# Products that nobody reads, put into TensorE's program at three places of a vision block (1 core, Trainium2)

## The chip, the cores and the metric

The kernel runs on one core of a Trainium2 chip. The metric is the device time of one execution in microseconds, lower is better. The engines of the core work in parallel and meet through semaphores: TensorE (PE; its weight loads are PEld), VectorE (DVE), ScalarE (ACT), GpSimd (POOL) and SyncE (SP), which issues the DMAs. Each engine takes its own instructions in the order written in the program.

## The reference

32 images of 3 x 96 x 96 are cut into patches of 16 x 16, which makes 36 tokens of 768 numbers for each image, 1152 tokens in all. Everything is float32.

```python
p = _layernorm(p, ln1_g, ln1_b)                       # 768 -> W_proj -> 192
h = _layernorm(einsum('bnd,de->bne', p, W_proj), ln2_g, ln2_b)
q, k, v = ...                                         # 8 heads of 24
attn = softmax(einsum('bnhd,bnhe->bhde', q/|q|, k/|k|) * temp)   # 24 x 24, over channels
h = layernorm(h + einsum('bhde,bnhe->bnhd', attn, v) @ W_proj + b)
logits = (h/|h|) . slots                              # 8 experts x 4 slots
D = softmax(logits, over tokens); C = softmax(logits, over slots)
H = gelu((D . h/|h|) @ W_down + b_down); Y = H @ W_up + b_up
out = layernorm(h + C . Y)
```

## The kernel before

The tokens are cut into 11 groups (`NG`) of three images, 108 tokens, the last of two images, 72 tokens. All buffers are in SBUF; `ps` is the PSUM tensor of eight banks. Each engine has one long program written out by hand.

**Head.** SyncE loads `b1`, `g1` and the token weights `wt`, then for each group the transposed input `xT` (for the products) and the plain input `xs` (for the statistics), with the other weights between. There are four buffers `xs`, so the load of group g from 4 on waits until `x_stats(g - 4)` has been made; the wait stands in SyncE's program behind the load of `xT` of the same group. TensorE's `offset` (L399) multiplies `b1` by `wt` and `column_means` (L407) multiplies the constant matrix `share`, 128 x 128 filled with 1/768 by GpSimd's first memset, by the scaled weights `wg`. VectorE subtracts the means and writes `wc` (L637). TensorE waits for it and then makes `token(g)` (L417), six products per group.

**Phase 1.** For the first nine groups (`P1`) TensorE makes `token(g)` and `turn_h(g - 2)`, while VectorE makes `x_stats` (L649), `x_moments`, `token_out`, `token_stats` and `ln2_norm` in order. GpSimd makes the roots.

**Loop.** Then 17 steps s interleave the stages of different groups on TensorE: `values(s-2)`, `project(s-3)`, `logits(s-5)`, `qk(s)`, `turn_dc(s-6)`, `turn_l(s-5)`, `turn_h`, `token`, `gram(s-1)`, `mix(s-2)`, `turn_xn(s-4)`, `slot_in(s-6)`, `norms(s)`. A stage whose group is not between 0 and 10 is left out, so the last steps are thin: from step 12 on, `qk`, `gram` and `norms` are gone; step 15 has `logits(10)`, `turn_dc(9)`, `turn_l(10)` and `slot_in(9)`, and step 16 has `turn_dc(10)` and `slot_in(10)`. `gram` writes bank 3, which VectorE's `scores` reads and marks with `e2_scaled`. `hidden(0)` and `hidden(1)` (the experts' first product, L554) stand at the end of steps 13 and 14.

The stages that the change touches wait as follows. `turn_xn(g)` (L507) waits for `xn(g)` of VectorE; `slot_in(g)` (L542) waits for `dm(g)` of VectorE and `cT(g)` of ScalarE. In ScalarE's program `take_c(s-6)` is first in a step and `take_slots(s-6)` last, and `gelu(0)` (a table load and eight activations, L1026) stands at the end of step 15, in front of `take_c(10)`.

**End.** After the loop TensorE makes `slot_out(0)`, `slot_out(1)`, `hidden(2)`, and then for each group `slot_out(g)` (L565, writes bank 2 + g % 2) and `combine(g-2)` (L578). VectorE adds and makes the statistics of the last norm, GpSimd the root, ScalarE the result, and SyncE writes it out.

Of the kernel before, what the change touches and what calls it, by code (L numbers as in the profile page):

```python
# [35 lines left out]
NG = (B + GI - 1) // GI  # L36
# [14 lines left out]
def at(stage, g, first=0):  # L51

    if first <= g < NG:
        stage(g)
# [6 lines left out]
def tokens(g):  # L61
    return images(g) * TOK


def build(nc, x, x_t, w_tok, ln1_g, ln1_b, ln2_g, ln2_b, g2col, b2col, w_qk, w_v, w_proj, b_proj, temp, slots, scale,
          w_down, b_down, w_up, b_up, ident_h, imgsel_h, negmask_h, out):
    ctx = ExitStack()
    with ctx:
        def sb(name, shape):
            return ctx.enter_context(nc.sbuf_tensor(name, shape, F32))  # L70

        def sem(name):
            return ctx.enter_context(nc.semaphore(name))
# [11 lines left out]
        share = sb("share", [128, 128])  # L85
# [87 lines left out]
        ps = ctx.enter_context(nc.psum_tensor("ps", [128, 8, 512], F32))  # L173

        def csp():
            return ps[:, 0, 0:D]

        def bwp():
            return ps[:, 1, 0:D]
# [49 lines left out]
        def hp(b, ni):  # L229
            return ps[:, b % 2, 0:2 * ni * NP].rearrange("p (e i s) -> p e i s", e=2, i=ni)  # L230
# [30 lines left out]
        share_set = sem("share_set")  # L261
# [29 lines left out]
        e2_scaled = sem("e2_scaled")  # L291
# [51 lines left out]
        @block.sync  # L343
        def _(sp):
            def load_x(g):
                n = tokens(g)
                o = g * GI * TOK * KC
                sp.dma_start(xT[:, o:o + KC * n], x_t[:, o:o + KC * n]).then_inc(xT_in[g], 16)
                if g >= NB:
                    sp.wait_ge(st1_ready, g - NB + 1)  # L350
                sp.dma_start(xs[0:n, g % NB, :], x[g * GI * TOK:g * GI * TOK + n, :]).then_inc(x_in[g], 16)

            sp.dma_start(g1[:, :], ln1_g).then_inc(ln1_in, 16)
            sp.dma_start(b1[:, :], ln1_b).then_inc(ln1_in, 16)
            sp.dma_start(wt[:, :, :], w_tok.rearrange("(k p) e -> p k e", p=128)).then_inc(wtok_in, 16)
            load_x(0)
            sp.dma_start(ident[:, :], ident_h).then_inc(ident_in, 16)
            load_x(1)
            load_x(2)
            sp.dma_start(g2[:, :], g2col).then_inc(ln2_in, 16)  # L360
            sp.dma_start(b2[:, :], b2col).then_inc(ln2_in, 16)
            sp.dma_start(wqk[:, :, :, :, :].rearrange("p f j h d -> p f (j h d)"), w_qk).then_inc(wqkv_in, 16)
            sp.dma_start(wv[:, :, :, :].rearrange("p f h d -> p f (h d)"), w_v).then_inc(wqkv_in, 16)
            load_x(3)
            sp.dma_start(g2row[:, :], ln2_g.partition_broadcast(128)).then_inc(rows_in, 16)
            sp.dma_start(b2row[:, :], ln2_b.partition_broadcast(128)).then_inc(rows_in, 16)
            sp.dma_start(bprow[:, :], b_proj.partition_broadcast(128)).then_inc(rows_in, 16)
            sp.dma_start(imgsel[:, :], imgsel_h).then_inc(masks_in, 16)
            sp.dma_start(negmask[:, :], negmask_h).then_inc(masks_in, 16)
            sp.dma_start(tempc[:, :], temp).then_inc(attn_in, 16)  # L370
            sp.dma_start(wp[:, :, :], w_proj).then_inc(attn_in, 16)
            for g in range(4, NG):
                load_x(g)
            sp.dma_start(spraw[:, :, :, :].rearrange("p f n q -> p f (n q)"),
                         slots.rearrange("(f p) n q -> p f (n q)", f=2)).then_inc(slots_in, 16)
            sp.dma_start(scl[:, :], scale.broadcast_to([F, 1])).then_inc(slots_in, 16)
            sp.dma_start(wd[:, :, :, :].rearrange("p f n h -> p f (n h)"), w_down).then_inc(experts_in, 16)
            sp.dma_start(bd[:, :], b_down).then_inc(experts_in, 16)
            sp.dma_start(bu[:, :], b_up).then_inc(experts_in, 16)
            sp.wait_ge(cleared, 6)  # L380
            for j in range(4):
                sp.dma_start(wu[32 * j:32 * j + HID, :, :], w_up[j]).then_inc(experts_in, 16)

            ov = out.rearrange("b n d -> (b n) d")
            for g in range(NG):
                sp.wait_ge(o4_ready, g + 1)
                sp.dma_start(ov[g * GI * TOK:g * GI * TOK + tokens(g), :],
                             o4[0:tokens(g), g % NQ, :]).then_inc(out_done[g % NQ], 16)
            for i in range(NQ):
                sp.wait_ge(out_done[i], 16 * len(range(i, NG, NQ)))  # L390


        @block.tensor
        def _(pe):
            def offset():
                pe.wait_ge(ln1_in, 32)
                pe.wait_ge(wtok_in, 16)
                for kc in range(KC):
                    mm = pe.matmul(bwp(), b1[:, kc:kc + 1].broadcast_to([128, 128]), wt[:, kc, :],  # L399
                                   start=kc == 0, stop=kc == KC - 1)  # L400
                mm.then_inc(bwp_ready, 1)

            def column_means():
                pe.wait_ge(share_set, 1)
                for kc in range(KC):
                    pe.wait_ge(wg_ready, kc + 1)
                    mm = pe.matmul(csp(), share[:, :], wg[:, kc, :], start=kc == 0, stop=kc == KC - 1)  # L407
                mm.then_inc(csp_ready, 1)
# [137 lines left out]
            def hidden(b):  # L546
                i0, i1 = HB[b][0] * GI, min(B, HB[b][1] * GI)
                pe.wait_ge(xt_ready, HB[b][1])
                if b >= 2:
                    pe.wait_ge(hb_ready, b - 1)  # L550
                for n in range(NE):
                    j = n % 4
                    for f in range(2):
                        mm = pe.matmul(hp(b, i1 - i0)[32 * j:32 * j + HID, n // 4, :, :], wd[:, f, n, :],  # L554
                                       xt[:, f, i0:i1, n, :], start=f == 0, stop=f == 1,
                                       tile_position=(0, 32 * j))
                mm.then_inc(hp_ready, 1)

            def slot_out(g):
                i0, ni = g * GI, images(g)  # L560
                pe.wait_ge(hb_ready, 1 + sum(g >= e for _, e in HB[:-1]))
                if g >= 2:
                    pe.wait_ge(yt_ready, g - 1)
                for e in range(2):
                    mm = pe.matmul(ytp(g), hb[:, e, i0:i0 + ni, :, :].rearrange("p i n q -> p (i n q)"),  # L565
                                   wu[:, e, :], start=e == 0, stop=e == 1)
                mm.then_inc(ytp_ready, 1)

            def combine(g):
# [6 lines left out]
                if g >= 2:  # L576
                    pe.wait_ge(z2_ready, g - 1)
                pe.matmul(yop(g), cT[0:images(g) * SL, g, 0:tokens(g)], yt[0:images(g) * SL, g % NQ, :],  # L578
                          start=True, stop=True).then_inc(yop_ready, 1)

            offset()
            column_means()
            pe.wait_ge(wc_ready, 1)
            for g in range(P1):
                token(g)
# [8 lines left out]
            for s in range(17):  # L594
                at(values, s - 2)
                at(project, s - 3)
                at(logits, s - 5)
                at(qk, s)
                at(turn_dc, s - 6)
                at(turn_l, s - 5)  # L600
                at(turn_h, s + P1 - 2 - 1, P1 - 2)
                at(token, s + P1 - 1, P1)
                at(gram, s - 1)
                at(mix, s - 2)
                at(turn_xn, s - 4)
                at(slot_in, s - 6)
                at(norms, s)
                if s == NG + 2:
                    pe.wait_ge(experts_in, 16 * (3 + 4))
                    pe.wait_ge(qk_ready, NG)  # L610
                    hidden(0)
                if s == NG + 3:
                    pe.wait_ge(v_ready, NG)
                    hidden(1)
            pe.wait_ge(lnn_ready, NG)
            pe.wait_ge(e2_scaled, NG)
            slot_out(0)
            slot_out(1)
            hidden(2)
# [610 lines left out]
```

## Time and profile before

| | |
|---|---|
| median of 3 runs | 141.82 us (139.89 to 144.46) |
| the profiled execution | 140.0 us, span 138.0 us |
| mean granted TensorE clock | 0.939 |
| TensorE matmul busy | 115.0 us (83%), 1779 instructions |
| VectorE busy | 88.9 us (64%) |
| ScalarE busy | 69.0 us (50%) |
| GpSimd busy | 67.0 us (49%) |
| read from HBM, written | 9.17 MB, 0.88 MB |

The span is the time from the first to the last instruction of the profiled execution; the time of that execution is 2.0 us longer. Line numbers are those of the kernel before. One product in float32 shows as two weight loads (PEld) and two matmuls (PE). The granted clock is given as a share of 2.4 GHz.

### The profile page before, as it was taken

The numbers are of one execution on the slowest core, as the hardware profiler recorded it, in microseconds if no ns is written. First come the engines' busy times: TensorE is split into PE (matmuls) and PEld (weight loads), VectorE is DVE, ScalarE is ACT, GpSimd is POOL, SyncE is SP. The second block draws the span as 40 slices with busy tenths as digits, with TensorE's granted clock in tenths as the row PEclk, the third lists the DMA queues.
The fourth block names the chain that finished last, engine by engine and source line by source line (L and its number), as shares of the span: only waits on it lengthen the run. The fifth ranks groups of instructions, "written<-read, shape, count | busy, mean of one in ns | idle before, by whom it ended". The sixth has DMA issues, their size and how long they took to land.

```text
span 138.0 us, 4819 instructions
## 1 busy us (share of the span) xinstructions
PE 115.0 (83%) x1779; PEld 93.6 (68%) x1779; DVE 88.9 (64%) x380; ACT 69.0 (50%) x234; POOL 67.0 (49%) x158
## 2 busy tenths in 40 slices
PE   0297799999699999999999999997986860999920
PEld 0297799888377868578787796866964630788700
DVE  0211999999643687985857558586987440159980
ACT  3000004242862848648675686846644468763553
POOL 8500277767847428837265382743664000007871
PEclk9999999999999999999999999999999555599995
DMA  1999899988000000000000000000000000000232
GB/s 14 337 293 278 269 305 320 314 319 214 5 7 0 5 0 7 5 0 7 0 5 5 0 5 0 10 5 0 5 0 7 0 0 0 5 0 24 72 89 71
DMA packets 7677, 10.34 MB, mean 75 GB/s; under 512 B 2056, under 2 KB 5032, under 8 KB 7656
## 3 DMA queue, kind: packets, MB, share of 16 engines
q1 hardware_dynamic: 7656, 10.06, 24.2%
q8 instruction: 14, 0.23, 0.7%
q14 instruction: 7, 0.06, 0.1%
HBM read 9.17 MB, written 0.88 MB: 73 GB/s over the span
## 4 chain that ended last, share of the span: by engine, by line
PE 47%; DVE 22%; issue 12%; POOL 10%; ACT 4%; DMA 3%; SPq 1%; POOLq 1%; DVEq 0%; ACTq 0%
DVE st L649 8%; PE ps L565 7%; PE ps L436 6%; PE ps L476 5%; PE ps L496 3%; PE ps L542 3%; PE ps L399 3%; DMA wt<-in_w_tok 3%; PE ps L489 3%; PE ps L519 3%; DVE y L663 3%; PE ps L578 3%; DVE st L671 2%; PE ps L507 2%; PE ps L407 2%
## 5 line engine op out<-in xcount | busy, mean ns | idle before, releaser
L417 PE MATMUL ps<-wc,xT 128*108 128x192 f32 (+1 forms) x132 | 23.0, 327 | 1.5 <-DVE wc L637 1.5
L940 ACT ACTIVATE hT<-ps,b,g 96x108 f32<-96x108 f32 (+1 forms) x22 | 8.4, 430 | 27.9 <-PE ps L426 27.9
L417 PEld LDWEIGHTS ps<-wc,xT 128*108 128x108 f32 (+1 forms) x132 | 20.7, 170 | 2.0 <-DVE wc L637 1.8
L436 PE MATMUL ps<-wqk,hT 96*108 96x384 f32 (+1 forms) x44 | 16.2, 490 | 0.7 <-ACT qp L962 0.7
L1125 POOL TENSOR_SCALAR pw<-mv 108x1 f32<-108x1 f32 (+1 forms) x11 | 3.7, 337 | 21.3 <-DVE mv L780 21.3
L476 PE MATMUL ps<-hT,wv 96*128 96x108 f32 (+1 forms) x88 | 12.5, 284 | 0.0
L1139 POOL TENSOR_SCALAR var<-mv 108x1 f32<-108x1 f32 (+1 forms) x11 | 2.4, 223 | 18.9 <-DVE mv L875 18.4
L950 ACT ACTIVATE sq<-ps 108x384 f32<-108x384 f32 (+1 forms) x11 | 5.4, 490 | 12.4 <-PE ps L436 12.4
L476 PEld LDWEIGHTS ps<-hT,wv 96*128 96x128 f32 x88 | 10.7, 191 | 0.7
L649 DVE BATCH_NORM_STATS2 st<-xs 108x6 f32<-108x384 f32 (+1 forms) x22 | 10.9, 540 | 0.2 <-issue 0.2
L960 ACT ACTIVATE km<-ps,imgsel 108x192 f32<-108x192 f32 (+1 forms) x32 | 11.0, 418 | 0.0
L565 PE MATMUL ps<-wu,hb 128*96 128x192 f32 (+1 forms) x44 | 10.6, 375 | 0.0
L542 PE MATMUL ps<-dm,xn 108*96 108x96 f32 (+1 forms) x44 | 6.7, 284 | 3.9 <-ACT cT L1013 3.9
L1082 POOL TENSOR_SCALAR var<-mv 108x1 f32<-108x1 f32 (+1 forms) x11 | 2.4, 222 | 15.3 <-DVE mv L655 15.3
L436 PEld LDWEIGHTS ps<-wqk,hT 96*108 96x108 f32 (+1 forms) x44 | 6.8, 171 | 4.1 <-issue 1.6
L1035 ACT ACTIVATE o<-z,sh,rstd 108x192 f32<-108x192 f32 (+1 forms) x11 | 6.0, 546 | 6.4 <-DVE sh L880 6.4
L399 PE MATMUL ps<-wt,b 128*128 128x192 f32 x12 | 4.2, 538 | 6.0 <-DMA wt<-in_w_tok 6.0
L496 PE MATMUL ps<-wp,yT 128*108 128x192 f32 (+1 forms) x44 | 9.1, 330 | 0.0
L542 PEld LDWEIGHTS ps<-dm,xn 108*96 108x96 f32 (+1 forms) x44 | 5.6, 194 | 4.3 <-issue 3.6
L834 DVE RECIPROCAL rC<-sC 108x1 f32<-108x1 f32 (+1 forms) x11 | 1.8, 162 | 10.3 <-ACT eD L1006 10.3
L565 PEld LDWEIGHTS ps<-wu,hb 128*96 128x96 f32 (+1 forms) x44 | 7.3, 184 | 1.5 <-issue 0.7
L399 PEld LDWEIGHTS ps<-wt,b 128*128 128x128 f32 x12 | 3.7, 333 | 5.9 <-issue 5.9
(106 smaller groups left out, 304.6 us busy)
## 6 DMA issues: line engine op xcount, KB each, us to landing
xT<-in_x_t SPq DMA_DIRECT2D x10, 324.0 KB, 7.0
xs<-in_x SPq DMA_DIRECT2D x10, 324.0 KB
out<-o SPq DMA_DIRECT2D x10, 81.0 KB
wt<-in_w_tok SPq DMA_DIRECT2D x1, 576.0 KB, 4.2
wqk<-in_w_qk SPq DMA_DIRECT2D x1, 288.0 KB, 8.7
xT<-in_x_t SPq DMA_DIRECT2D x1, 216.0 KB, 7.5
xs<-in_x SPq DMA_DIRECT2D x1, 216.0 KB
wv<-in_w_v SPq DMA_DIRECT2D x1, 192.0 KB, 9.0
```

The source lines that it names most:

```text
L399: mm = pe.matmul(bwp(), b1[:, kc:kc + 1].broadcast_to([128, 128]), wt[:, kc, :], start=kc == 0, stop=kc == KC - 1)
L417: mm = pe.matmul(tokp(g), xT[:, o + kc * n:o + (kc + 1) * n], wc[:, kc, :], start=kc == 0, stop=kc == KC - 1)
L436: mm = pe.matmul(qkp(g), hT[:, f, t0:t0 + tokens(g)], wqk[:, f, :, :, :].rearrange("p j h d -> p (j h d)"), start=f == 0, stop=f == 1)
L476: mm = pe.matmul(vp(g)[:, m, :], wv[:, f, 4 * m:4 * m + 4, :].rearrange("p h d -> p (h d)"), hT[:, f, t0:t0 + tokens(g)], start=f == 0, st ...
L496: mm = pe.matmul(prp(g), yT[:, g % NY, m, 0:images(g), :].rearrange("p i n -> p (i n)"), wp[:, m, :], start=m == 0, stop=m == 1)
L542: mm = pe.matmul(xtlp(g)[:, f, :], xn[0:tokens(g), g, f * F:(f + 1) * F], dm[0:tokens(g), g % NX, 0:images(g) * SL], start=True, stop=True)
L565: mm = pe.matmul(ytp(g), hb[:, e, i0:i0 + ni, :, :].rearrange("p i n q -> p (i n q)"), wu[:, e, :], start=e == 0, stop=e == 1)
L649: ins = dve.bn_stats(st1[0:n, g % 2, h, :], xs[0:n, g % NB, h * (PD // 2):(h + 1) * (PD // 2)])
L940: ins = act.activation(hT[:, f, t0:t0 + tokens(g)], htp(g)[:, f, :], ACT.Identity, bias=b2[:, f:f + 1], scale=g2[:, f:f + 1])
L950: act.activation(sq[0:n, g % 2, :, :, 0:DH].rearrange("p j h d -> p (j h) d"), p, ACT.Square).then_inc(sq_ready, 1)
L960: act.activation(km[0:n, g % NK, i, :], qkp(g)[:, D:2 * D], ACT.Copy, scale=imgsel[0:n, i:i + 1])
L1035: act.activation(o4[0:n, g % NQ, :], z2[0:n, g % NQ, :], ACT.Identity, bias=sh4[0:n, g:g + 1], scale=rstd4[0:n, g:g + 1]).then_inc(o4_read ...
```

## The change

TensorE gets a helper that multiplies `share` by itself, 128 x 128 by 128 x 128, into bank 3, and nobody reads the result. It stands at these places:
- 11 products at the start of the program, behind a new wait for `share_set` (the memset of `share`);
- 3 products between `column_means` and the wait for `wc`;
- in each of the loop steps 12 to 16, 3 products in front of `turn_xn` and 3 in front of `slot_in` (in steps 15 and 16 there is no `turn_xn`, so that six stand together);
- 6 products after the loop, in front of `slot_out(0)`.

The wait for `e2_scaled` of all groups, which stood behind the loop, moves into step 12, since the products write the bank that `scores` reads.

```diff
+            def keep_busy(count, bank):
+                for _ in range(count):
+                    pe.matmul(ps[:, bank, 0:128], share[:, :], share[:, :], start=True, stop=True)
+
...
+            pe.wait_ge(share_set, 1)
+            keep_busy(11, 3)
             offset()
             column_means()
+            keep_busy(3, 3)
             pe.wait_ge(wc_ready, 1)
...
                 at(mix, s - 2)
+                if s == NG + 1:
+                    pe.wait_ge(e2_scaled, NG)
+                if s > NG:
+                    keep_busy(3, 3)
                 at(turn_xn, s - 4)
+                if s > NG:
+                    keep_busy(3, 3)
                 at(slot_in, s - 6)
                 at(norms, s)
...
+            keep_busy(6, 3)
             pe.wait_ge(lnn_ready, NG)
-            pe.wait_ge(e2_scaled, NG)
             slot_out(0)
```

## Rows read from the trace of the kernel before

**Rows 1.** The page's 40 slices of 3.45 us, busy tenths, clock and DMA.

```profile
PE   0297799999699999999999999997986860999920
PEclk9999999999999999999999999999999555599995
DMA  1999899988000000000000000000000000000232
GB/s 14 337 293 278 269 305 320 314 319 214 5 7 0 5 0 7 5 0 7 0 5 5 0 5 0 10 5 0 5 0 7 0 0 0 5 0 24 72 89 71
```

**Rows 2.** Waits of TensorE: us in total, times, longest us.

```profile
PE ps L399 <- DMA wt<-in_w_tok: 6.0, 1, 6.0
PE ps L542 <- ACT cT L1013: 3.9, 2, 3.4
...
PE ps L417 <- DVE wc L637: 1.5, 1, 1.5
```

**Rows 3.** Windows, TensorE alone: us, busy (instructions), granted clock, DMA.

```profile
36.00:40.00 4.00, 2.89 (x51) 1.00 0.01 4
...
100.00:104.00 4.00, 2.99 (x52) 1.00 0.00 0
104.00:108.00 4.00, 2.75 (x48) 0.94 0.02 6
112.00:116.00 4.00, 1.04 (x6) 0.50 0.00 0
116.00:120.00 4.00, 3.01 (x12) 0.50 0.02 4
```

**Rows 4.** Timeline of the head: start us, us, engine, line, operation.

```profile
0.72 0.20 POOL L1068 MEMSET share<- 128x128 f32 x1 [0.29 <-POOLq L1187]
...
5.96 4.18 PE L399 MATMUL ps<-wt,b 128*128 128x192 f32 x12 [5.96 <-DMA wt<-in_w_tok]
...
13.17 1.35 DVE L637 TENSOR_TENSOR wc<-wg,ps 128x1152 f32<-128x1152 f32 x1 [5.76 <-PE ps L407]
...
14.58 3.66 PE L417 MATMUL ps<-wc,xT 128*108 128x192 f32 x21 [1.52 <-DVE wc L637]
```

**Rows 5.** Timeline of narrow stretches, for the distance between starts.

```profile
6.74 0.85 PE L399 MATMUL ps<-wt,b 128*128 128x192 f32 x2
...
42.27 0.50 PE L476 MATMUL ps<-hT,wv 96*128 96x108 f32 x3
```

**Rows 6.** Issue and landing of an input block, and the chain at x_stats(4).

```profile
11.74 1.12 SPq L348 DMA_DIRECT2D xT<-in_x_t  x1
...
xT<-in_x_t SPq DMA_DIRECT2D x1, 324.0 KB, 8.6
...
22.69 0.91 DVE st L649 x2
```

**Rows 7.** Timeline of TensorE in loop steps 12 to 16.

```profile
101.25 0.39 PE L507 MATMUL ps<-ident,xn 108*96 108x108 f32 x2 [0.18 <-DVE xn L803]
...
104.92 0.39 PE L507 MATMUL ps<-ident,xn 108*96 108x108 f32 x2 [0.57 <-DVE xn L803]
...
107.80 0.48 PE L507 MATMUL ps<-ident,xn 72*96 72x72 f32 x2 [0.28 <-DVE xn L803]
...
111.57 0.93 PE L542 MATMUL ps<-dm,xn 108*96 108x96 f32 x4 [0.49 <-ACT cT L1013]
...
116.99 0.88 PE L542 MATMUL ps<-dm,xn 72*96 72x64 f32 x4 [3.44 <-ACT cT L1013]
```

**Rows 8.** The chain that ended last, from the table load on: start us, us.

```profile
112.88 1.28 ACT L1026
...
117.87 2.61 PE ps L565 x8
120.48 0.59 PE ps L554 x32
121.08 0.90 PE ps L565 x4
```

## The prediction

> **What bounds the kernel now.** I read the page by slices first. TensorE is busy nine tenths or more in most of them, the granted clock stands at full until slice 31, at half in slices 32 to 35, and the DMA engines are nearly full from slice 1 to 9 and then empty [rows 1]. So there are three regimes. In the head, TensorE waits 6.0 us for the token weights and the input stream fills the DMA queues. In the middle, TensorE is the chain. At the end its in-order program stops for other engines. The waits of TensorE name the stops: 6.0 us for the weights at L399, 1.5 us for the centred weights at L417, and 3.9 us at L542, 3.4 of it in one piece, for a copy that ScalarE makes behind the first gelu [rows 2].
>
> The clock is next. The windows give it as 1.00 in 100 to 104 and 0.50 in 112 to 120; it fell late in 104 to 108, after stretches in which TensorE was busy 2.99 and 2.75 of 4 us, and was back at full from about 121.2 after some 3.4 us of back-to-back products from 117.8 on [rows 1, 3, 8]. [...] The head shows 1.00 as well, but its products tell otherwise: two starts of L399 are 0.85 - 0.53 = 0.32 us apart, which is 2 x 192 columns at 1.2 GHz, and L417 passes 21 of the same width in 3.66 us, 0.16 us each [rows 4, 5]. The head runs at the lower level until about 12 us; no record before the first change of clock exists there, and the 1.00 of the view is a default, as I read it.
>
> **Price of a product.** Each fp32 product here is two weight loads and two matmuls. The nearest row for "128 columns of weights, 128 streamed" is L476 (128 and 108): three starts span 0.50 us, the last lasts 0.275, so 0.112 us from start to start. Its 108 streamed columns alone would take 0.09, so the load of 128 columns, the same as here, sets it [rows 5]. From below, 2 x 128 columns at 2.4 GHz give 0.107; from above, L399's 192 columns give 0.16. I take 0.112: a product costs 0.22 us at full clock and 0.44 at half. So three cost 0.67 or 1.3, six 1.34 or 2.7, eleven 2.5 or 4.9.
>
> **Head.** `share` is set at 0.92 [rows 4]. Eleven products at the lower level run from 1.0 to 5.9 at most; the weights are there at 5.96 [rows 4]. They cost nothing, and would cost at most 0.1 us. If they lift the clock by 6 us, L399 takes 12 x 0.16 = 1.9 us for 4.2, L407 ends near 10.0 in place of 13.1, and VectorE's `wc` (13.17, 1.35 us) and the first token product move up by 3.0 us. The three products after `column_means` (0.67) lie in TensorE's wait of 1.5 us for `wc` [rows 2, 4]. Cover gone, they would cost 0.67.
>
> How much of the 3.0 us lives on? The input stream stands against it. The transposed block 4 is issued at 11.74 and lands 8.6 us later, at 20.3; the plain block 4 is next in the queue, 324 KB at about 300 GB/s, 1.1 us, so it lands at about 21.4 to 21.8 [rows 1, 6]. VectorE reads it at 22.69 in `x_stats(4)` [rows 6]. It can be read about 1.0 us earlier, not 3.0: VectorE will stand in front of `x_stats(4)` for about 2 us. Behind it the blocks come every 2.1 us and VectorE takes 2.2 a group, so no more is lost. Bounds: 0.8 if the landing is 21.8, 3.0 if the queue, filled earlier, were also emptied earlier. Queues that are full leave little of that. I take **-1.0**, and everything up to the loop's last steps moves by it.
>
> What the lower level in the head is can be set beside a page. The Trainium skill, "TensorE: Matmul & The Clock Gate", Part 1, says that the low clock is the default and activity releases it, which is what the 0.32 and 0.16 us show. The same part says that the ramp costs under 1% of a typical span; by that the head could give back at most 1.4 us here, against 3.0 from the products and 1.0 after the stream. That sides with the smaller number.
>
> **Loop steps 12 to 16.** TensorE issues in order, so products ahead of `turn_xn` and `slot_in` delay all behind them unless TensorE would have waited. The wait on `e2_scaled` costs nothing: the scores of the last group are step 11's work on VectorE, and `mix(10)`, just ahead in step 12, needs what is made from them. At step 12, `turn_xn(8)` stood at 101.25 after a wait of 0.18 [rows 7]; with three products it stands at 101.65, and `slot_in(6)`, 101.48 before, at 102.55: +1.07. `project(10)`, `logits(8)` and `turn_dc(7)` sit behind it. VectorE takes the logits 0.5 later, since it was busy. In step 13 `turn_xn(9)` (104.92 after 0.57 idle [rows 7]) slips by 0.5, `logits(9)` by 1.2, and VectorE's mask and `unit_h1(10)` by 1.0. In step 14 `turn_xn(10)` (107.80) comes at 109.0: +1.2 [rows 7].
>
> From there the clock pays back. If it stays at full, `slot_in(8)` and `hidden(1)` and `logits(10)` take 1.3 us where they took 2.1, even with three products (0.67) between, so `lm(10)` is late by 0.8, not 1.9. Step 15 has six products in one place, 1.34 us, ahead of `slot_in(9)`, which waited 0.49 for its input [rows 7]: it starts 1.4 late, takes 0.34 + drain for 0.93, and ends 1.0 late. ScalarE's table load and `gelu(0)`, 112.88 to 116.6 [rows 8], move by +1.0, and so does `slot_in(10)`, from 116.99 to 118.0. The six products of step 16 lie in its wait of 3.44 us [rows 7] and cost nothing; if that cover went they would cost 1.34.
>
> **In front of the experts' outputs.** `slot_out(0)` has all its inputs when `slot_in(10)` ends, so six products stand fully on the path: +1.34. But the two `slot_out` after them took 2.61 us at half clock [rows 8] and take 1.3 at full, and `slot_in(10)` saves 0.45. `slot_out(2)`, at 121.08 [rows 8], would start at 118.0 + 0.3 + 1.34 + 1.3 + 0.4 (`hidden(2)`) = 121.35. From there to the end nothing is added and the clock is full in both, so this part is **+0.3**, clock kept. If the products bought no clock it would be far more (below).
>
> **Will the clock stay?** Steps 12 to 15 gain 1.34 us of products each, so 2.99 and 2.75 busy become nearly 4, above anything that lost it [rows 3]. But between the last product of step 16 (115.7) and `slot_in(10)` (118.0) TensorE is idle 2.3 us. Before, 1.5 us idle at L417 left the clock up, and 3.4 us stand in a stretch already low, so the answer lies between [rows 2, 3]. If it falls there, it falls in front of the densest part; the only row for its return is the 3.4 us of back-to-back work before 121.2, half of which is lost: +1.7. I give 0.6 to a fall and take **+1.0**.
>
> **Sum.** 140.0 (span 138.0 and 2.0 around it) - 1.0 + 0.3 + 1.0 = 140.3 against the profiled execution. That execution lies 1.8 under the median of 141.82; the three runs and the profiled one average 141.5. I cannot see in one trace what the slower ones lost. Part may be clock, which the products protect, part the input stream, which they don't. I add half, 0.8 to 0.9: **141.2**.
>
> **Rivals.**
> A, forecast (0.50): head capped by the stream, products nearly pay for themselves, half clock for one dense stretch: 139.0 to 143.0.
> B, faster (0.30): the clock holds through the gelu gap and the first input blocks do land earlier, or the slow ones of the runs before were clock. With 2.0 from the head, 140.0 - 2.0 + 0.3 = 138.3. For it: 144.46 against 139.89 is a spread that the clock could make. Against it: DMA near full from 4 us on [rows 1].
> C, slower (0.14): the clock falls near 107 all the same, because what counts is not TensorE's busy time. Then the products run at 0.44. `slot_in(8)` is 3.0 late, six products at half clock ahead of `slot_in(9)` make it 4.9, six ahead of `slot_out(0)` 7.6, less about 1 for an earlier return: 140.0 - 1.0 + 6.6 = 145.6. It decides if the granted clock is 0.5 before 113. For it: a stretch of 2.99 was near a fall and one of 2.89 was not, so busy time is a poor measure.
> D (0.06): the clock holds, but nothing of the head survives the stream, and the products cost what they save: within 0.5 of before.
>
> **Chances and range.** About 2% is what a measurement of this kernel can tell. Faster than 139.0 needs B or the lower edge of A: 0.24. Slower than 144.7 is C and a rest of A: 0.15. Between, 0.61. The range takes A with its bounds, most of B and not the core of C: 138.0 to 144.2. The likeliest case's own range is 139.0 to 143.0.
>
> **What would show it.** Starts of L399 0.16 us apart; `wc` near 10.2; VectorE idle about 2 us in front of `x_stats(4)`, read at 21.5 to 21.8; `turn_xn(10)` some 1.2 later relative to the loop; a granted clock of 1.00 to at least 115; table load of `gelu(0)` near 113.9 less 1.0; 1.34 us of products directly ahead of L565. A first `x_stats(4)` under 21, or a clock of 0.5 before 113, makes the prediction wrong, the one to the fast side and the other to the slow.

## The result: slower by 3.5%

| | before | changed |
|---|---|---|
| median | 140.85 us (139.43 to 144.46, 4 runs) | 144.68 us (143.05 to 148.24, 4 runs) |
| ratio | | 1.0346, 95% interval 1.0247 to 1.0445 |
| profiled execution, span | 140.0, 138.0 | 144.64, 142.6 |
| mean granted clock | 0.939 | 0.963 |
| TensorE busy | 115.0 us | 125.2 us |

I had predicted 141.2 (138.0 to 144.2), with 139.0 to 143.0 as the likeliest case. The mean clock did rise, and the kernel got slower. Ratios here leave out executions well above the fastest of their kernel; medians are of all, and by them the change costs 2.7%.

The busy slices and the clock of the changed kernel, to be held against [rows 1]:

```profile
PE   7997975699699999999999999998999983999920
PEclk9999999999959999999999999999999999599995
DMA  2999998886000000000000000000000000000222
```

Four slices at half clock near the end have become one. It is the fall in front of the dense part (the experts' outputs behind the loop), to which the prediction gave 0.6. A new one stands in the twelfth slice, 39.2 to 42.8 us, at the start of the loop. The 3.45 us slices of before are 3.57 us here.

The waits of the changed kernel, us in total, times, longest, for [rows 2]:

```profile
DVE st L662 <- DMA xs<-in_x: 3.5, 3, 1.5
...
PE ps L546 <- ACT cT L1026: 2.2, 1, 2.2
```

VectorE waits 3.5 us for the plain input, which it did not do at all in the profile of the kernel before. The wait behind the gelu is shorter only because products fill its first part.

The head in the timeline (start us, us), for [rows 4]:

```profile
0.98 4.90 PE L397 MATMUL ps<-share 128*128 128x128 f32 x22 [0.98 <-POOL share L1081]
...
6.09 2.19 PE L403 MATMUL ps<-wt,b 128*128 128x192 f32 x12 [0.20 <-DMA wt<-in_w_tok]
8.11 2.11 PE L411 MATMUL ps<-wg,share 128*128 128x192 f32 x12
10.06 0.83 PE L397 MATMUL ps<-share 128*128 128x128 f32 x6
10.33 1.35 DVE L650 TENSOR_TENSOR wc<-wg,ps 128x1152 f32<-128x1152 f32 x1 [2.81 <-PE ps L411]
...
11.74 6.10 PE L421 MATMUL ps<-wc,xT 128*108 128x192 f32 x36 [0.85 <-DVE wc L650]
```

Step by step what the prediction said: 4.9 us of products, done just before the weights; L403 in 2.19 us for 4.18; `wc` at 10.33 for 13.17; the token products 2.8 us earlier.

The same stretch further on, where the gain goes. VectorE's reads of blocks 4 and 5, for the 22.69 of [rows 6]:

```profile
22.36 1.02 DVE L662 BATCH_NORM_STATS2 st<-xs 108x6 f32<-108x384 f32 x2 [1.45 <-DMA xs<-in_x]
...
25.75 1.02 DVE L662 BATCH_NORM_STATS2 st<-xs 108x6 f32<-108x384 f32 x2 [1.07 <-DMA xs<-in_x]
...
35.26 1.50 PE L440 MATMUL ps<-wqk,hT 96*108 96x384 f32 x4
38.67 1.84 PE L440 MATMUL ps<-wqk,hT 96*108 96x384 f32 x4 [0.66 <-ACT qp L975]
...
40.66 3.33 PE L421 MATMUL ps<-wc,xT 128*108 128x192 f32 x12
```

(The 22.69 stands in the view of the chain; the timeline of the kernel before has these reads at 22.61 and 24.81.) Block 4 is read 0.3 us earlier than before, where the prediction said 21.5 to 21.8, block 5 at 25.75 for 24.81, and the first `qk` (L440, step 0) starts at 35.26; in the kernel before it stood at 34.28:

```profile
34.28 1.50 PE L436 MATMUL ps<-wqk,hT 96*108 96x384 f32 x4
...
39.23 2.12 PE L417 MATMUL ps<-wc,xT 128*108 128x192 f32 x12
```

2.8 us of lead have become 1.0 us of delay. Then the clock falls, and one token group takes 3.33 us for 2.12.

The loop's end and the experts, for [rows 7, 8]:

```profile
104.20 0.35 PE L511 MATMUL ps<-ident,xn 108*96 108x108 f32 x2
...
107.82 0.39 PE L511 MATMUL ps<-ident,xn 108*96 108x108 f32 x2
...
111.46 0.29 PE L511 MATMUL ps<-ident,xn 72*96 72x72 f32 x2
...
115.50 0.50 PE L546 MATMUL ps<-dm,xn 108*96 108x96 f32 x4
...
116.75 1.55 PE L397 MATMUL ps<-share 128*128 128x128 f32 x12
120.49 0.52 PE L546 MATMUL ps<-dm,xn 72*96 72x64 f32 x4 [2.19 <-ACT cT L1026]
120.85 2.15 PE L397 MATMUL ps<-share 128*128 128x128 f32 x12
122.79 2.58 PE L569 MATMUL ps<-wu,hb 128*96 128x192 f32 x8
125.30 0.46 PE L558 MATMUL ps<-xt,wd 96*24 96x32 f32 x32
125.70 0.89 PE L569 MATMUL ps<-wu,hb 128*96 128x192 f32 x4
```

And the windows, TensorE alone (us, busy, granted clock, DMA), for [rows 3]:

```profile
36.00:40.00 4.00, 2.68 (x47) 0.96 0.03 7
100.00:104.00 4.00, 3.83 (x62) 1.00 0.02 4
...
116.00:120.00 4.00, 1.79 (x14) 1.00 0.00 0
120.00:124.00 4.00, 3.51 (x20) 0.70 0.00 0
124.00:128.00 4.00, 4.00 (x51) 0.87 0.00 0
```

The clock stayed at full through steps 12 to 15, and it fell at 121.6, behind the wait for the gelu and just in front of the dense part. It stayed up there in all five profiled kernels that have products in these steps. In the nine without them it fell between 104.9 and 116.6, in four before 109 (before, half_x_head, wait_only, six_only) and in five after 111: where the kernel before lost it, at 107.6, is not where every execution does.

**Where the 4.6 us of span come from**, profile against profile. First `qk`: +1.0. Clock at half near 40 (the second to the third `qk`: 38.67 to 45.70, 7.0 us, before 37.70 to 43.05, 5.35): +1.7. By step 12 this has shrunk a little, `slot_in(5)` is 2.4 late (100.02 for 97.60). `slot_in(10)` is 3.5 late (120.49 for 116.99): +1.1 from the loop's products. The third `slot_out` is 4.7 late (125.70 for 121.01): +1.2 from the six products and the half clock, less what full clock saved. From there nothing changes. So head and early loop +2.4, end +2.3, and 140.0 + 4.7 = 144.7 for the 144.64 measured.

### The profile page after: what moved, and what is told of

It reads as the page before. It is cut to its first block, busy times and chain, and to the rows that moved or that the text cites. A ratio compares the mean times of both kernels' runs of the same rounds, so it can differ in the third digit from the quotient of the medians.

```text
span 142.6 us, 5019 instructions
## 1 busy us (share of the span) xinstructions
PE 125.2 (88%) x1879; PEld 104.3 (73%) x1879; DVE 89.6 (63%) x380; ACT 69.3 (49%) x234; POOL 66.8 (47%) x158
## 2 busy tenths in 40 slices
DMA packets 7679, 10.36 MB, mean 73 GB/s; under 512 B 2057, under 2 KB 5033, under 8 KB 7657
## 4 chain that ended last, share of the span: by engine, by line
PE 56%; DMA 11%; issue 10%; DVE 9%; POOL 6%; ACT 5%; SPq 1%; POOLq 0%; ACTq 0%; DVEq 0%
DMA xs<-in_x 8%; PE ps L440 8%; PE ps L569 6%; PE ps L397 5%; PE ps L480 5%; PE ps L500 4%; PE ps L493 3%; DMA wt<-in_w_tok 3%; PE ps L523 3%; DVE st L662 3%; PE ps L546 3%; PE ps L421 3%; PE ps L582 2%; PE ps L511 2%; PE ps L469 2%
## 5 line engine op out<-in xcount | busy, mean ns | idle before, releaser
L421 PE MATMUL ps<-wc,xT 128*108 128x192 f32 (+1 forms) x132 | 24.2, 338 | 0.8 <-DVE wc L650 0.8
L421 PEld LDWEIGHTS ps<-wc,xT 128*108 128x108 f32 (+1 forms) x132 | 21.9, 179 | 1.4 <-DVE wc L650 1.0
L440 PE MATMUL ps<-wqk,hT 96*108 96x384 f32 (+1 forms) x44 | 16.5, 497 | 0.7 <-ACT qp L975 0.7
L397 PE MATMUL ps<-share 128*128 128x128 f32 x100 | 16.2, 318 | 1.0 <-POOL share L1081 1.0
L397 PEld LDWEIGHTS ps<-share 128*128 128x128 f32 x100 | 14.9, 230 | 1.0 <-POOL share L1081 1.0
L569 PE MATMUL ps<-wu,hb 128*96 128x192 f32 (+1 forms) x44 | 10.3, 367 | 0.0
L440 PEld LDWEIGHTS ps<-wqk,hT 96*108 96x108 f32 (+1 forms) x44 | 6.8, 171 | 4.1 <-issue 1.6
L868 DVE TENSOR_TENSOR yt<-ps,bu 96x192 f32<-96x192 f32 (+1 forms) x11 | 3.6, 328 | 7.9 <-PE ps L569 7.9
L569 PEld LDWEIGHTS ps<-wu,hb 128*96 128x96 f32 (+1 forms) x44 | 7.3, 182 | 1.5 <-issue 0.8
L1039 ACT ACTIVATE hb<-ps,bd 24x48 f32<-24x48 f32 (+1 forms) x24 | 6.9, 288 | 2.4 <-PE ps L558 2.1
```

What stands on the lines that cost most here:

```text
L397: pe.matmul(ps[:, bank, 0:128], share[:, :], share[:, :], start=True, stop=True)
L421: mm = pe.matmul(tokp(g), xT[:, o + kc * n:o + (kc + 1) * n], wc[:, kc, :], start=kc == 0, stop=kc == KC - 1)
L440: mm = pe.matmul(qkp(g), hT[:, f, t0:t0 + tokens(g)], wqk[:, f, :, :, :].rearrange("p j h d -> p (j h d)"), start=f == 0, stop=f == 1)
L1039: ins = act.activation(hb[r, n // 4, i0:i1, n, :], hp(b, i1 - i0)[r, n // 4, :, :], ACT.Gelu, bias=bd[r, n // 4:n // 4 + 1])
```

## The experiments

Twelve kernels ran, in four groups, each beside its own executions of the kernel before. The medians of the kernel before were 140.61, 139.39, 140.80 and 140.02 us. The theory after the traces: the end costs 2 us as rows say (T), and in the head the input stream takes back what the clock gave (S).

### The change in parts

**head_only.** The changed kernel with the products of the loop and of the end taken out.

```diff
             pe.wait_ge(share_set, 1)
             keep_busy(11, 3)
             offset()
             column_means()
             keep_busy(3, 3)
...
-                if s == NG + 1:
-                    pe.wait_ge(e2_scaled, NG)
-                if s > NG:
-                    keep_busy(3, 3)
                 at(turn_xn, s - 4)
-                if s > NG:
-                    keep_busy(3, 3)
                 at(slot_in, s - 6)
...
-            keep_busy(6, 3)
             pe.wait_ge(lnn_ready, NG)
+            pe.wait_ge(e2_scaled, NG)
```

> Only the 11 + 3 products of the head. In the trace of the changed kernel the plain input block 5 was issued at 14.59 in place of 17.00 and VectorE got it at 25.75 in place of 24.90, so the first step of phase 2 came 1.1 us later although the first token product came 2.8 us earlier. Theory S (the input stream: loads issued earlier share the engines and the needed block lands later): VectorE waits again some 3 us in all in front of x_stats(3) to x_stats(5), x_stats(5) not before 24.9, and the time is equal to before or up to 1.5 us longer (ratio 1.000 to 1.010). Theory N (the late block 5 was a chance of that one execution; the head gives back 1.0 us as predicted): x_stats(5) near 23.9, ratio 0.990 to 0.995.

Measured: 140.47 us (138.47 to 146.96, 6 runs) beside 140.61; ratio 0.989 (0.983 to 0.996). The two do not say the same: three executions lie at 138.5 to 139.4 and three at 141.6 to 147.0. By the ratio theory N fits and S (1.000 to 1.010) does not; by the medians, 0.999, the head brings nothing. The waits of VectorE in this kernel:

```profile
DVE st L656 <- DMA xs<-in_x: 3.1, 3, 1.4
```

3.1 us again, as S says. `x_stats(5)` stood at 24.55, between the two theories' figures. Alone it settles nothing; the pair below does.

**tail_only.** The changed kernel with those of the head taken out.

```diff
-            pe.wait_ge(share_set, 1)
-            keep_busy(11, 3)
             offset()
             column_means()
-            keep_busy(3, 3)
+            pe.wait_ge(share_set, 1)
```

> Only the products of loop steps 12 to 16 and the six in front of slot_out(0). Theory T (products on the path cost 0.5 + 0.6 us up to slot_in(9), six more 1.3 to 2.0 us, less what the clock gives back): 1.3 to 3.0 us longer than before, ratio 1.010 to 1.021, with the clock at 1.00 to at least 115 and the start of slot_out(2) that much later relative to step 12. Rival (the loss of the changed kernel sits in the head and the early loop, the tail pays for itself): ratio 0.995 to 1.005.

Measured: 143.21 us (141.79 to 147.79) beside 140.61; ratio 1.015 (1.008 to 1.022), by the medians 1.018. T holds: by the medians most of the loss is here, and the rival's 1.000 is outside. Its clock was 1.00 in 100 to 120 and 0.70 in 120 to 124, with the same 1.79 us busy in 116 to 120 as in the changed kernel.

**no_six.** The changed kernel less one line:

```diff
-            keep_busy(6, 3)
             pe.wait_ge(lnn_ready, NG)
```

> The changed kernel without the six products in front of slot_out(0). They stood from 120.85 to 122.8 in the chain. Theory T: 1.3 us less than the changed kernel if the clock is full there and 2.0 to 2.7 less if it is half, so a ratio to before of 1.015 to 1.025 for 1.035 with them. Rival (they bring the clock back sooner for the dense part behind, as their place suggests): no gain, 1.03 to 1.04.

Measured: 142.15 us (139.33 to 146.79) beside 140.61, by the medians 1.011, where the changed kernel has 1.027. That is below T's 1.015 to 1.025, and a weak number: the executions are six, and no ratio is on record. The difference of the medians, 1.6% or 2.3 us, is T's for half clock. The profiles give less: from the start of `slot_in(10)` to the third `slot_out` they take 5.21, 5.19 and 5.21 us with the six (changed, after_2, tail_only) and 3.71 without, so 1.5 us. The rival, no gain, is not borne out by either. The six give back little to the part behind; the clock was back at 125.1, 124.2 and 125.0 with them and at 123.9 without:

```profile
120.12 0.57 PE L546 MATMUL ps<-dm,xn 72*96 72x64 f32 x4 [2.20 <-ACT cT L1025]
120.49 2.83 PE L569 MATMUL ps<-wu,hb 128*96 128x192 f32 x8
```

This is the timeline of no_six: L569 follows at once, eight matmuls in 2.83 us, so at half clock as in [rows 8]; in the changed kernel the same eight took 2.58.

**six_only.** The kernel before with only those six.

```diff
             column_means()
+            pe.wait_ge(share_set, 1)
...
+            pe.wait_ge(e2_scaled, NG)
+            keep_busy(6, 3)
             pe.wait_ge(lnn_ready, NG)
-            pe.wait_ge(e2_scaled, NG)
```

> Only the six products in front of slot_out(0). Theory T (they stand fully on the path, and the clock is at half when they start, as in the kernel before): 2.6 us added, some 1.1 us given back because the clock returns while they run, so +1.0 to +1.6 us, ratio 1.007 to 1.012; slot_out(2) near 122.5 for 121.0. Rival (they pay for themselves): 0.997 to 1.003.

Measured: 141.21 us (140.32 to 143.18) beside 140.80; ratio 1.015 (1.006 to 1.024), by the medians 1.003. The sign is T's, the size is uncertain. Timeline:

```profile
118.33 2.88 PE L397 MATMUL ps<-share 128*128 128x128 f32 x12
121.00 2.03 PE L569 MATMUL ps<-wu,hb 128*96 128x192 f32 x8
```

Six products at half clock take 2.7 us; L569, in which the clock comes back, takes 2.03 for 2.82. `slot_out(2)` stood at 123.35, but `slot_in(10)` was already 0.67 late (117.66), so 1.7 us are the products'. With no_six's 1.5 this is the firmest price of the six: 1.5 to 1.7 us in the profiles.

### Is it the stream?

**half_x and half_x_head.** The plain input's load is cut to half its columns and read twice, once without and once with the head's products.

```diff
-                sp.dma_start(xs[0:n, g % NB, :], x[g * GI * TOK:g * GI * TOK + n, :])
+                sp.dma_start(xs[0:n, g % NB, 0:PD // 2], x[g * GI * TOK:g * GI * TOK + n, 0:PD // 2])
...
-                    ins = dve.bn_stats(st1[0:n, g % 2, h, :], xs[0:n, g % NB, h * (PD // 2):(h + 1) * (PD // 2)])
+                    ins = dve.bn_stats(st1[0:n, g % 2, h, :], xs[0:n, g % NB, 0:PD // 2])
```

> No products at all. The load of the plain input brings only the first 384 of 768 columns of each row, and both statistics instructions read that half, so the result is not the reference's; VectorE's work is the same, the stream carries 1.8 MB less. This is the partner of half_x_head. If the stream already bounds the kernel before in most executions (theory S; x_stats(9) waited for its block at 34.6 to 35.4 in three kernels, and was free at 34.0 in the profiled one of before), the time is 0 to 1.5 us below before: ratio 0.990 to 1.000.

> half_x (the plain input's second half is not loaded, the first is read twice) with the 11 + 3 products of the head. Theory S (the head's products do lift the clock and bring wc forward by 1.3 to 2.9 us, but the input stream takes it back): with the stream out of the way x_stats waits for nothing, x_stats(9) stands near 31.1, and the kernel is 1.5 to 3 us faster than half_x (ratio between the two 0.98 to 0.99). Rival P (the products themselves, or something else early in the loop, eat the gain): no difference between the two although VectorE waits for no input.

Measured: half_x 139.33 us (138.79 to 139.84, 12 runs), half_x_head 137.27 us (135.74 to 138.63, 6 runs), before 139.39. Ratios to before 1.002 (0.999 to 1.005), a little above what was expected, and 0.983 (0.976 to 0.991). With the stream out of the way the same fourteen products are worth 2.06 us, a ratio of 0.985 between the two. No wait for `xs` stands in VectorE's list of either. Timelines, first of half_x, then of half_x_head:

```profile
34.01 1.50 PE L436 MATMUL ps<-wqk,hT 96*108 96x384 f32 x4
```

```profile
10.47 1.35 DVE L644 TENSOR_TENSOR wc<-wg,ps 128x1152 f32<-128x1152 f32 x1 [2.80 <-PE ps L411]
...
31.59 1.50 PE L440 MATMUL ps<-wqk,hT 96*108 96x384 f32 x4
```

`wc` starts at 10.47, as in the changed kernel (10.33), against 12.89 in half_x, and the first `qk` is at 31.59 against 34.01: the whole lead of 2.4 us lives. That is theory S, shown. It shows too that the stream alone does not hold the kernel before: half_x is no faster. There token products, statistics and stream all go at some 2.2 us a group, and the stream lies just behind.

The profiled kernels with the full input say the same. The lists are in the order before, tail_only, fill_wait, wait_only, six_only, wait_only_2 (no products in the head) and changed, head_only, no_six, after_2, head_wait, head_late (products in the head):

| | without | mean | with | mean |
|---|---|---|---|---|
| `wc` starts, us | 13.17, 11.66, 11.97, 13.24, 12.11, 12.58 | 12.46 | 10.33, 10.30, 10.23, 10.42, 10.81, 10.08 | 10.36 |
| VectorE waits for `xs`, us | 0, 2.2, 2.5, 0, 1.8, 0 | | 3.5, 3.1, 3.2, 3.6, 1.0, 1.9 | |
| first `qk`, us | 34.28, 33.74, 34.23, 34.33, 34.21, 33.69 | 34.08 | 35.26, 34.03, 34.86, 34.78, 33.05, 33.22 | 34.20 |

The table shows one thing more. Without products in the head the clock rose by itself, between 9.0 and 12.1 us, and `wc` moved with it by 1.6 us. The products bring `wc` forward by 2.1 us on the mean; the 2.8 of the first pair had one of the latest heads to compare with. And in the three kernels whose `wc` came earliest by itself VectorE waited for the stream too, and the first `qk` was no earlier for it.

**head_late.** Why did block 5 come at 25.75 in the changed kernel, later than before, though it was issued at 14.59 in place of 17.00?

```diff
                 if g >= NB:
-                    sp.wait_ge(st1_ready, g - NB + 1)
+                    sp.wait_ge(st1_ready, g - NB + 2)
```

> head_only with one edit on SyncE: the load of plain block g waits for x_stats(g - 3) in place of x_stats(g - 4), so that fewer loads are in flight. Theory Q (crowding: block 5 landed at 25.7, 24.3, 25.3 and 25.2 in the four kernels with head products, which issue it near 14.6, and at 23.8, 24.2, 24.7, 24.1 in the four without, which issue it at about 17; loads in flight together take turns from each other): block 5 lands before 24.5 and the time is 0.3 to 1 us below head_only. Rival (the stream is late because of its bytes, not its order): issuing later only lands later, block 5 at 25 or more, and the time is equal or up to 1.5 us longer than head_only.

Measured: 140.82 us (137.48 to 142.87) beside 140.80, by the medians 1.000, as head_only (0.999). The ratio, 1.012 (1.001 to 1.022), is not used: one execution stands at 137.48, the other five at 139.62 and more. Block 5 landed at 22.7, as Q says, but the time is not shown to be below head_only, and head_wait (below), which issues block 5 when the changed kernel does, had it at 23.3. So in the five kernels of the unchanged order the landing lies anywhere between 23.3 and 25.7, and Q is not shown. What makes a block late stays open.

### A better place

**fill_wait.** No head; steps 12 to 15 as in the change; fifteen products in the gelu wait, none behind.

```diff
                 if s > NG:
-                    keep_busy(3, 3)
+                    keep_busy(12 if s == NG + 5 else 3, 3)
                 at(slot_in, s - 6)
...
-            keep_busy(6, 3)
```

> No head products; steps 12 to 15 as in the change; in step 16 fifteen products in place of six (15 x 0.22 = 3.4 us, the length of the wait for gelu(0) before); none in front of slot_out(0). Theory T with the clock held through the wait: 1.3 us less on the path and no half-clock stretch (1.7) against tail_only, so ratio 0.990 to 1.003 to before, granted clock 1.00 up to the last output. Rival (the clock falls there all the same): the gain over tail_only is 1.3 us alone.

Measured: 141.29 us (138.93 to 148.94, 13 runs) beside 140.61; ratio 1.000 (0.994 to 1.006). Against tail_only, 143.21, it takes off 1.9 us and comes out even. The clock was 1.00 through the wait and the dense part (in 124 to 132). Products in steps 12 to 15 and in the wait together pay for themselves and no more. Its profiled execution lost some 7 us elsewhere (`slot_in(10)` at 127.89, where tail_only has 120.34): the clock was at half from 50.2 to 70.7, in the loop, where no product stands.

**wait_only, and again as wait_only_2.** Eight products in step 16 and no other.

```diff
+                if s == NG + 5:
+                    pe.wait_ge(e2_scaled, NG)
+                    keep_busy(8, 3)
                 at(slot_in, s - 6)
```

> Products only in step 16, eight of them, in TensorE's wait for gelu(0) (8 x 0.22 = 1.8 us at full clock, 8 x 0.44 = 3.5 at half); none in the head, in steps 12 to 15 or in front of slot_out(0). Theory T: nothing of it stands on the path; the clock falls near 107 to 113 as before, and the two slot_out and slot_in(10) run at full or get there sooner, 0.5 to 1.7 us less than before: ratio 0.988 to 0.997. Rival (eight products are not enough to bring the clock back in time, or they run over the end of the wait): 1.000 or up to 1.005.

> The kernel with eight products in step 16's wait and none elsewhere, a second time: its first interval, 0.979 to 1.000, just touches 1. Theory T: in the first profile everything up to slot_in(10) lay where it lay before (116.91 for 116.99) and slot_out(2) came 1.5 us sooner, so ratio 0.988 to 0.997 again. Rival (chance): 0.998 to 1.005.

Measured: 139.62 us (136.81 to 140.82) beside 139.39, ratio 0.990 (0.979 to 1.000), by the medians 1.002; again, 138.63 us (135.78 to 142.51) beside 140.02, by the medians 0.990. The twelve executions together have a median of 138.9, the 29 of before beside them 139.8. Timeline of the first:

```profile
113.27 3.71 PE L397 MATMUL ps<-share 128*128 128x128 f32 x16
116.91 0.87 PE L546 MATMUL ps<-dm,xn 72*96 72x64 f32 x4
117.58 1.65 PE L569 MATMUL ps<-wu,hb 128*96 128x192 f32 x8
...
119.55 0.89 PE L569 MATMUL ps<-wu,hb 128*96 128x192 f32 x4
```

Everything up to `slot_in(10)` lies within 0.1 us of the kernel before (116.91 for 116.99). The eight products fill the wait of 3.44 us at half clock, the clock is back at 117.9, and L569 takes 1.65 us for 2.82: `slot_out(2)` is 1.5 us sooner. Timeline of the second:

```profile
112.37 2.00 PE L397 MATMUL ps<-share 128*128 128x128 f32 x16
116.08 0.52 PE L546 MATMUL ps<-dm,xn 72*96 72x64 f32 x4 [1.71 <-ACT cT L1020]
116.44 2.71 PE L569 MATMUL ps<-wu,hb 128*96 128x192 f32 x8
...
119.67 1.01 PE L569 MATMUL ps<-wu,hb 128*96 128x192 f32 x4
```

Here the clock had not fallen before the wait. The same eight products took 2.00 us at full clock, TensorE stood idle for the remaining 1.71, the clock fell at 116.6, and L569 ran low: 2.71 us. head_wait's profile is alike (2.00, idle 1.71, fall at 116.4, L569 2.55). From the start of `slot_in(10)` to `slot_out(2)` the three take 2.64, 3.59 and 3.43 us, the kernel before 4.02. So the mechanism worked in one profile of three. A count that fills the wait at half clock does not fill it at full clock, and which of the two levels stands there differs between executions. The gain is small: the first interval reaches 1.000 and the second measurement has no interval.

**head_wait.** The same with the head's products.

> The head's 11 + 3 products and the eight in step 16's wait, nothing else. Theory (stream caps the head, wait-only products are free and take 1.0 to 1.5 us off the end): the head adds 0 to -0.7 us, so ratio 0.983 to 0.993, below before by 1.0 to 2.2 us. Rival (gains of head and tail add up in full, 2 us of the head among them): below 0.98.

Measured: 139.69 us (138.44 to 141.13, 12 runs) beside 140.80; ratio 1.002 (0.996 to 1.009), by the medians 0.992. The ratio is outside what the theory said, the medians at its upper edge. The head adds nothing to wait_only that these runs can tell.

**after_2.** The changed kernel again, beside the half_x pair.

> The changed kernel once more, beside the others. If its parts add up (head 0 to +1.0 us, tail +2.1 to +3.0 us), its ratio to before is 1.015 to 1.028 here; if the parts make each other worse it stays at 1.035.

Measured: 143.47 us (140.20 to 144.81) beside 139.39, by the medians 1.029, as the first time (1.027). The parts, by the medians, are -0.1% for the head and +1.8% for the end. About 1% is not in their sum, and by the ratios more (0.989 and 1.015 for the parts, 1.035 for the whole). It has the size of the fall of the clock near 40, but head_only fell there too in its profile, so whether the parts make each other worse stays open.

## Why the prediction was wrong

**The head, -1.0 us: this step failed.** Its first half was right to within 0.2 us. The sum then let block 4 land when it had landed before, at 21.4 to 21.8, and took it as the last block that could delay anything: "Behind it the blocks come every 2.1 us and VectorE takes 2.2 a group, so no more is lost." Neither held. In the traces of the kernel before and of the changed kernel the last parts of block 4 land at 21.8 and 22.3, those of block 5 at 23.8 and 25.7, though both blocks were issued over 2 us sooner in the changed kernel. It was not the slack of the blocks behind that was too small: in the kernel before, block 4 lay 0.9 us in front of VectorE's read and blocks 5 to 9 lay 1.0 to 2.0. The landings themselves moved. VectorE read block 4 at 22.36 and stood three times, 3.5 us in all, and the first `qk` came 1.0 later where 1.0 earlier was forecast. The bounds, 0.8 to 3.0 of gain, did not include a gain of nothing. Over twelve profiles it is nothing: first `qk` at 34.2 with the products and 34.1 without.

**The start of the loop: missing.** I had read the stretch 36 to 40 (busy 2.89, clock full [rows 3]) as one that kept the clock, and went on. In the changed kernel the clock fell at 39.7 in the same stretch, for +1.7 us. It fell between 37.9 and 39.8 in five of the six profiled kernels with head products and full input, and in one of the six without (two more fell at 50); in the half_x pair it fell there without the products (38.4) and not with them. Why the head makes it likelier, if it does, is not shown; the term belonged in the sum with its price and a chance, for before and after alike.

**The products of steps 12 to 15: right.** `turn_xn(8)`, `turn_xn(9)` and `turn_xn(10)` were to slip by 0.4, 0.5 and 1.2 relative to the loop. They slipped by 0.5, 0.5 and 1.2, taking 2.4 off 2.95, 2.9 and 3.66. `slot_in(9)` was to be 1.4 late and end 1.0 late; it started 1.5 late. `slot_in(10)`: +1.0 forecast, +1.1 measured. The distance between starts, 0.112 us, was right too: twelve matmuls in 1.55 us, of which the last takes some 0.3.

**In front of the experts' outputs: right in kind, too low.** Forecast +0.3 with the clock kept and +1.3 with a fall weighted by 0.6; measured 2.3 up to `slot_out(2)`. The fall came behind the wait, while the six products ran, and just ahead of the dense part as described. Given the fall, +0.3 and +1.7 make 2.0. So the mis-sized part is the weight: the wait for the gelu left TensorE idle for 2.19 us, and the clock fell after it in all four profiles that have six products in it (changed, after_2, tail_only, no_six), and after 1.71 us in wait_only_2 and head_wait. I should have counted it whole. The six products themselves took 1.95 us (120.85 to 122.79), since the clock fell while they ran, and not 1.34.

**The rivals.** C, the slower one, hung on a fall near 107, and the clock was 1.00 there and up to 121.6. Its 145.6 lies close to the measured 144.64 by luck: the clock was at half before 113 only from 39.7 to 43.1. That is the sign named for C, at a place that C did not mean. So the kernel came out slow by A's mechanisms: A with its head term at a loss, a whole fall at the gelu, and an early fall that no rival had. D (0.06) had the head right, nothing of it survives, but let the clock hold and the products pay. B failed on both its conditions: the clock fell behind the gelu's wait, and the input blocks did not land earlier.

**The page.** "TensorE: Matmul & The Clock Gate" of the Trainium skill, Part 1, puts the ramp at under 1% of a typical span. The half_x pair measured 2.06 of 139.3 us, 1.5%, with half of the plain input not loaded; there the measurement decides. In the kernel itself the ramp was worth nothing.

## What to carry to other kernels

A product that keeps the clock up is free only inside a wait that TensorE would have had anyway, with its whole length at the lower clock: eight in the gelu wait cost nothing, six behind it cost 1.5 to 1.7 us. Whether they buy anything depends on the level at which they run: eight took 1.2 us off the next two stages when they ran at half clock, and 0.1 to 0.3 when they ran at full and left the rest of the wait empty. Before a head start is booked as a gain, read the landing of every block of the stream behind it, take the smallest slack as the ceiling, and do not take the landings as fixed: here they moved by up to 2 us against the profile read first. A rise of the mean granted clock (0.939 to 0.963 here) is no measure of success.

## What the runs showed of the hardware

The granted clock in a view is 1.00 until its first record, whatever the level: in the kernel before, L399's starts are 0.32 us apart under a 1.00 [rows 5], and in the changed kernel they are half of that.

One fall can last. In fill_wait's profiled execution the clock stayed at half from 50.2 to 70.7, and the execution took 148.94 us; 138.93 was the fastest of the same kernel. Windows of it, TensorE alone (us, busy, granted clock, DMA):

```profile
46.00:50.00 4.00, 3.21 (x116) 1.00 0.02 4
50.00:54.00 4.00, 3.53 (x8) 0.52 0.00 0
54.00:58.00 4.00, 4.00 (x111) 0.50 0.02 4
...
70.00:74.00 4.00, 4.00 (x116) 0.92 0.02 6
```

TensorE is busy in the view for nearly all of it and gets no clock back, while in [rows 3] a stretch of 2.99 kept it. The busy column counts time in which any product runs, 96 small ones with weights of 32 x 32 (L493) among them; it is a poor guide to whether the clock returns. What in the mix kept it low is not shown. Nor is the spread between executions of one kernel all of this kind. Of the 63 executions of the kernel before, the two with the lowest mean clock (0.918 and 0.920) took 142.17 and 143.56 us, but one of 143.21 had 0.953 and one of 141.52 had 0.964.

The landing of the plain block 5 moved between 22.7 and 25.7 us over the twelve profiles with full input, in which it was issued between 14.2 and 17.1, with the DMA engines near full in all. I had treated the pace of a full stream as steady.
